# The Q, K, V projection of the next tile spread over steps 0 to 2 of an attention unit instead of 0 and 1

## The reference

```python
xn = _ln(x) * (1 + sc_msa[:, None, :]) + sh_msa[:, None, :]
qkv = xn @ w_qkv + b_qkv                      # 576 -> 3 x 16 heads x 36
q = _ln(q, g_q)                               # over the 36 entries of a head
k = _ln(k, g_k)
attn = softmax(einsum('bhqd,bhkd->bhqk', q, k) * HD ** (-0.5))
o = einsum('bhqk,bhkd->bhqd', attn, v) ... @ w_proj + b_proj
x = x + g_msa[:, None, :] * o
h = gelu((_ln(x) * (1 + sc_mlp) + sh_mlp) @ w1 + b1)
x = x + g_mlp[:, None, :] * (h @ w2 + b2)
```

## Time and profile before

| | us |
|---|---|
| median of three runs | 2977.52 (2975.45 to 2980.61) |
| the profiled execution's own time | 2975.9 |
| its span, first to last instruction | 2974.1 |
| PE busy | 2791.4 (94%) |
| DVE busy | 2008.1 (68%) |
| ACT busy | 1535.3 (52%) |
| POOL busy | 690.3 (23%) |

### The profile page before, as it was taken

One profiled execution on the slowest core, in us unless ns is written; L12 is line 12 of the kernel. 1 busy time (PEld: TensorE's weight loads), 2 busy tenths in 40 slices (PEclk: granted clock), 3 DMA queues, 4 the chain that ended last, 5 costly groups with the idle time before them and its releaser, 6 DMA issues. The chain is left out here.

```text
span 2974.1 us, 43644 instructions
## 1 busy us (share of the span) xinstructions
PE 2791.4 (94%) x14764; PEld 1441.4 (48%) x14764; DVE 2008.1 (68%) x2665; ACT 1535.3 (52%) x2211; POOL 690.3 (23%) x496
## 2 busy tenths in 40 slices
PE   4579999999999999999999999359999999999999
PEld 1334444444444444444444444126675766757666
DVE  5568888888888888888888899565344353443521
ACT  2457777778877777777777777342112111121110
POOL 0143256632233343333333310010000000000000
PEclk9789999999999999999999999669999999999999
DMA  5142223222211111111111100451202112021100
GB/s 168 64 84 52 53 65 82 72 64 50 50 37 34 31 31 33 29 34 28 34 28 33 30 13 14 146 166 34 80 7 85 54 32 85 9 78 54 33 17 17
DMA packets 201780, 157.00 MB, mean 53 GB/s; under 512 B 146982, under 2 KB 147494, under 8 KB 201522
## 3 DMA queue, kind: packets, MB, share of 16 engines
q1 hardware_dynamic: 199976, 152.17, 18.6%
q10 hardware_dynamic: 1676, 3.02, 0.3%
HBM read 87.49 MB, written 34.09 MB: 41 GB/s over the span
## 5 line engine op out<-in xcount | busy, mean ns | idle before, releaser
L705 DVE TENSOR_TENSOR at_plo<-at_p 128x1024 fp32r<-128x1024 f32 x1024 | 1266.9, 1257 | 215.8 <-ACT at_p L616 206.6
L616 ACT ACTIVATE at_p<-at_ps 128x1024 f32<-128x1024 f32 x1024 | 1048.3, 1026 | 424.9 <-PE at_ps L833 423.8
L845 PE MATMUL at_ps<-at_plo,at_vr 128*37 128x512 f32 x2048 | 1070.7, 590 | 0.0
L842 PE MATMUL at_ps<-at_p,at_v 128*73 128x512 bf16 x2048 | 796.3, 389 | 0.4 <-DVE at_plo L705 0.3
L1288 PE MATMUL ml_ps<-ml_w2s,ml_hid 128*128 128x288 f16 x3456 | 429.8, 287 | 2.0 <-issue 2.0
L1309 PE MATMUL ml_ps<-ml_xhi,ml_w 128*128 128x512 f16 x1296 | 400.9, 382 | 11.9 <-ACT ml_g L1139 9.0
L1288 PEld LDWEIGHTS ml_ps<-ml_w2s,ml_hid 128*128 128x128 f16 x3456 | 338.7, 98 | 87.9 <-issue 2.5
L842 PEld LDWEIGHTS at_ps<-at_p,at_v 128*73 128x73 f16 x2048 | 232.7, 114 | 239.8 <-DVE at_plo L705 1.7
L845 PEld LDWEIGHTS at_ps<-at_plo,at_vr 128*37 128x37 f32 x2048 | 233.6, 114 | 221.3
L525 POOL TENSOR_TENSOR at_tssq<-at_tssq,head_eps 128x8 f32<-128x8 f32 x112 | 124.1, 1108 | 925.2 <-DVE at_tssq L679 925.2
L861 PE MATMUL at_ps<-wq,at_xhi 128*128 128x432 f16 x1008 | 297.1, 350 | 19.1 <-DVE at_txc L683 18.6
(11 more groups left out here) (157 smaller groups left out, 2317.6 us busy)
## 6 DMA issues: line engine op xcount, KB each, us to landing
head_sums<-at_oT SPq DMA_DIRECT2D x256, 72.0 KB
ml_held<-head_sums SPq DMA_DIRECT2D x64, 256.0 KB
at_xy<-in_x SPq DMA_DIRECT2D x32, 288.0 KB, 2.8
ml_x<-in_x SPq DMA_DIRECT2D x8, 1152.0 KB, 5.6
out<-ml_x SPq DMA_DIRECT2D x7, 1152.0 KB, 4.5
wm<-in_L_cond_w_mod SPq DMA_DIRECT2D x6, 1152.0 KB, 14.3
ml_hid<-in_L_cond_w SPq DMA_DIRECT2D x5, 1152.0 KB, 5.6
ml_held<-head_rden SPq DMA_DIRECT2D x24, 216.0 KB
```

The source lines that it names most:

```text
L616: act.activation(p[:, s % NP, :], ps[:, 2 * (s % 2):2 * (s % 2) + 2, :].rearrange("p a n -> p (a n)"), ACT.Exp).then_inc(exp_done, 1)
L705: nc.vector.tensor_tensor(plo[:, s % NP, :], p[:, s % NP, :], high, ALU.subtract).then_inc(plo_ready, 1)
L842: nc.tensor.matmul(acc[0:VW, bass.ds((U % 2) * CH, CH)], v16[:, h % 2, 2 * s + a, 0:VW], high, start=(s == 0 and a == 0), stop=False, skip ...
L845: last = nc.tensor.matmul(acc[0:RW, bass.ds((U % 2) * CH, CH)], vr[:, h % 2, 2 * s + a, 0:RW], plo[:, s % NP, a * CH:(a + 1) * CH], start= ...
```

## The change

Three schedules written by hand are shifted. On PE the fourteen products of a tile stand in steps 0, 1 and 2 as 5, 5 and 4, where they stood in steps 0 and 1 as 7 and 7. On ACT `tile_v` moves from step 2 to 3 and `tile_square` from 3 to 4. On DVE `tile_sum` moves from step 3 to 4 and `tile_normal` from 6 to 7. POOL's `tile_power` follows by its semaphore. The number of instructions, their operands and their waits stay as they are.

```diff
 (ACT)
-                    if fresh and s == 2:
+                    if fresh and s == 3:
                         tile_v(X, row)
-                    if fresh and s == 3:
+                    if fresh and s == 4:
                         tile_square(X)
 (DVE)
-                    if fresh and s == 3:
+                    if fresh and s == 4:
                         tile_sum(X)
-                    if fresh and s == 6:
+                    if fresh and s == 7:
                         tile_normal(X)
 (PE)
-                    if fresh and s < 2:
-                        tile_products(U + 1, ..., range(7 * s, 7 * s + 7))
+                    if fresh and s < 3:
+                        tile_products(U + 1, ..., range(5 * s, min(5 * s + 5, 14)))
```

More of the change, by code:

```diff
@@ L934, in attend @@
                         sums(U - 1, (h - 1) % GH if fixed and qc == 0 else h, s - LAG + STEPS)
-                    if fresh and s < 2:
-                        tile_products(U + 1, 0 if at_end else u + 1, G + (2 if at_end else 1), range(7 * s, 7 * s + 7))
+                    if fresh and s < 3:
+                        tile_products(U + 1, 0 if at_end else u + 1, G + (2 if at_end else 1), range(5 * s, min(5 * s + 5, 14)))
                     if G == HATS_IN and s == 4:
```

## The result

The changed kernel takes 3090.11 us (median of four runs, 3088.46 to 3091.39) against 2978.39 for the kernel before, measured in alternation with it: 1.0375 times as long, 95% interval 1.0357 to 1.0393. That is 111.7 us; 108.8 were forecast. (The forecast of 3086 counted from 2977.52, the median of the first three runs before; a fourth makes it 2978.39.) The profiled execution of the changed kernel takes 3091.4 us.

The account below looks back on a forecast made before the run. PE, laid end to end, bounds the kernel. Terms of 71.8 + 17.8 + 18.2 + 1.0 = 108.8 us on the profiled 2975.9 give 3084.7, and 1.6 more for the median gives 3086 us, range 3068 to 3106.

Parts of the forecast that it names:

- What bounds the kernel; the slack: Attention: PE's work is laid end to end; a plain unit has 0.19 us to spare between normalisation and next product.
- The change on PE: Products in steps 0 to 2: step 3 keeps its distance from the first product; one more switch per unit costs 1 us.
- The later sum: DVE's sum, now behind the subtraction of step 4, starts 1.11 us later in a plain unit.
- The two paths: From sum to normalisation: through POOL it starts at 1209.19, through DVE behind step 7's subtraction at 1209.04; the later counts.
- plain (groups 1, 3 to 6): 78 plain units: PE waits 0.92 us in step 0 of each, 71.8 us.
- group 0: 16 tiles with no slack left: the whole 1.11 us of the later sum reaches PE, 17.8 us.
- group 2: 16 tiles: step 7's subtraction delays the normalisation by one pitch of 1.14 us, and PE waits already: 18.2 us.
- That POOL is not what ends last: Plain units: the power takes 1.64 us, DVE's path decides with a wait of 0.77 us; 3075 us, chance 0.15.
- That POOL shuts DVE out: Step 7's subtraction is lengthened by 0.72 us or held until the power ends: 3131 or 3173 us, chance 0.07.
- That every fourth unit collides with `head`: In 27 units `head` on POOL runs beside normalisation and gain, 19 us on top: 3106 us, chance 0.06.
- Not slower: Earlier scores 1 and 2 carry through to steps 4 and 7, so PE would not wait: 2973 us, chance 0.02.

Follow-up runs that it names:

- experiment 7: Kernel before with one more POOL addition of 128x8, result unused, in front of its own: 3054.25 us, ratio 1.0257.
- experiment 1: Kernel before with only PE's products spread as 5, 5, 4 over steps 0 to 2, ACT and DVE as before: 2976.74 us, ratio 0.9997.
- experiment 3: Changed kernel with the normalisation back behind the subtraction of step 6, sum and square still one step late: 3052.14 us, ratio 1.0249.
- experiment 5: Changed kernel with POOL's addition and power replaced by one addition of constants, normalisation behind the subtraction of step 7: 3078.13 us, ratio 1.0334.
- experiment 6: Changed kernel with POOL's addition and power replaced by one addition of constants and the normalisation behind the subtraction of step 6: 2975.85 us, ratio 0.9993.
- experiment 4: Changed kernel with the products as 7 and 7 in steps 1 and 2, so the first product is later too: 2971.00 us, ratio 0.9973.

## Why the prediction was right

**What bounds the kernel; the slack.** Right. PE back to back with 0.19 us to spare in a plain unit: experiment 7 measures it at 0.22 by lengthening one path, and the changed kernel itself gives 0.22 as well (1.11 by the later sum and 0.09 by the longer power, of which 0.98 arrive).

**The change on PE.** Costed at 1 us; experiment 1 finds 1.2 us less than before with 0 inside the interval, so no run shows this term. The step that mattered, that step 3 keeps its distance from the first product, holds.

**The later sum.** Forecast 1.11 us. From the tile's first load to the sum it is now 1268.38 - 1258.90 = 9.48; before it was 8.39 (1203.83 less the load of that tile at 1195.44): 1.09 in this unit, 1.11 in the mean of the plain ones.

**The two paths.** Right in both parts. In plain units POOL ends last; experiments 3, 5 and 6 show each path by itself. DVE's would end 0.25 earlier by experiment 5, where 0.15 were forecast (the idle 0.16 in front of the normalisation is less than that, since in these rows the normalisation starts 0.09 before the subtraction ends when nothing holds it). The term that was a little too small lies here: the power takes 2.59 instead of 2.50, and sum to normalisation 4.34 instead of 4.25. The prediction had what it takes to see it. It found that the power would start 0.13 into subtraction 6, as it starts inside subtraction 5 today, and took the same 2.50. Today it starts 0.22 into it, and what is left of the subtraction counts (see the hardware section).

**The terms.** They can be read off as distances between first product loads, from that of tile 1 to that of tile 111. Before:

```profile
184.75 0.13 PEld L861 LDWEIGHTS at_ps<-wq,at_xhi 128*128 128x128 f16 x2 [16.42 <-DVE at_txc L683]
...
1679.83 0.11 PEld L861 LDWEIGHTS at_ps<-wq,at_xhi 128*128 x2 [0.34 <-issue]
```

After:

```profile
187.25 0.13 PEld L861 LDWEIGHTS at_ps<-wq,at_xhi 128*128 128x128 f16 x2 [16.42 <-DVE at_txc L683]
...
260.88 0.11 PEld L861 LDWEIGHTS at_ps<-wq,at_xhi 128*128 x2 [1.54 <-issue]
275.52 0.11 PEld L861 LDWEIGHTS at_ps<-wq,at_xhi 128*128 x2 [1.54 <-issue]
...
698.55 0.11 PEld L861 LDWEIGHTS at_ps<-wq,at_xhi 128*128 x2 [1.71 <-issue]
713.79 0.11 PEld L861 LDWEIGHTS at_ps<-wq,at_xhi 128*128 128x128 f16 x2 [1.61 <-DVE at_txc L683]
...
1792.25 0.11 PEld L861 LDWEIGHTS at_ps<-wq,at_xhi 128*128 x2 [1.32 <-issue]
```

1605.00 against 1495.08: 109.9 us in 110 units. By the same distances at the ends of the groups:

| | units | forecast | measured |
|---|---|---|---|
| plain (groups 1, 3 to 6) | 78 | 71.8 | 76.3 |
| group 0 | 16 | 17.8 | 17.5 |
| group 2 | 16 | 18.2 | 16.1 |
| products cut in three | | 1.0 | in the above |

The plain term was 6% too small, 0.98 us a unit against 0.92: 0.09 by the longer power, less what every fourth unit saves (its load follows the normalisation by 0.05 and not by 0.15, as at 713.79 above, behind a normalisation that ends at 713.74). In group 3 the load follows by 0.24 or more in most units (941.10 behind a normalisation that ends at 940.85), some 1 us in all; the first product waits for one more semaphore there (`n_lo`), and whether that is why was not tried. The term of group 2 was 2 us too large, because it took an ordinary unit for all sixteen. Before the change every fourth one was already some 0.5 us longer; after it all take 15.2 to 15.3 us. The subtraction in front of the normalisation shows where the 0.5 came from. Beside two casts of `head` it takes 1.76 us in such a unit, 1.23 otherwise:

```profile
657.63 1.76 DVE L705 TENSOR_TENSOR at_plo<-at_p 128x1024 fp32r<-128x1024 f32 x1 [1.06 <-ACT at_p L616]
...
657.64 0.67 POOL L518 CAST at_v<-at_v 128x576 f16<-128x576 f32 x1
```

The plain term was thus 4.5 us too small and the other three together 3.4 too large. That the sum comes within 1.1 us of the 109.9 is in part luck. Of the 115.5 us between the two spans, 2.5 lie ahead of the first of these loads and 3.1 behind the last; what they are was not tried. The medians are 111.7 apart: the profiled execution before lies 2.5 us under its median and the one after 1.3 above, so some of it is the scatter between runs.

**The rivals.** That POOL is not what ends last: no, the power was 2.59 and not 1.64. Without the power the loss would be 12 us smaller, close to the 11 at which this rival was priced, but only because `head` then collides (experiment 5). That POOL shuts DVE out: no; the three subtractions up to the normalisation take 3.81 us, of which 0.14 are the wait for exponential 7. That every fourth unit collides with `head`: no, in the plain groups of the changed kernel those are not longer than the others. Before the change in group 2, and in experiment 5, some are, by 0.5 and 0.4 us. Not slower: no; exponential 7 starts 11.37 behind the tile's first load (1270.27 and 1258.90), where it started 11.39 behind it before (1206.83 and 1195.44), and experiment 4 shows what it takes, a later first product.

## What to carry to other kernels

A schedule that shifts a chain of hand-overs by a step has to shift its first consumer as well: here the reader of a single PSUM bank went one step later, and the next writer of the bank did not, so some 0.2 us of slack in 78 units, and none in 32, met 1.1 us of delay. Before moving a step for balance, look for the resource that closes the loop and subtract the end of its last reader from the start of its next writer: that difference, taken from one unit's timeline, predicted the loss within 3%, with some luck in how the errors of the terms fell. And where two paths of nearly the same length lead to a wait, shortening one gives back only the difference between them (12 of 112 us here), so both have to be costed before either is blamed.

## What the runs showed of the hardware

A POOL operation that starts within a DVE subtraction takes longer, by about what is left of the subtraction. In group 2 after the change the addition of 128x8 found DVE between subtractions and took 0.20 us; in plain units, beside one, it takes 1.11:

```profile
708.07 0.45 DVE L679 TENSOR_REDUCE at_tssq<-at_txc 128x8 f32<-128x288 f32 x1
708.70 1.23 DVE L705 TENSOR_TENSOR at_plo<-at_p 128x1024 fp32r<-128x1024 f32 x1 [0.19 <-ACT at_p L616]
...
708.59 0.20 POOL L525 TENSOR_TENSOR at_tssq<-at_tssq,head_eps 128x8 f32<-128x8 f32 x1 [6.33 <-DVE at_tssq L679]
708.87 2.55 POOL L527 TENSOR_TENSOR at_tssq<-at_tssq,power 128x8 f32<-128x8 f32 x1
```

The power then starts at 708.87, within the subtraction at 708.70, and takes 2.55 where it took 1.64 before the change in this group. The subtractions in which the power starts in a plain unit, before and after the change:

```profile
1205.32 1.22 DVE L705 TENSOR_TENSOR at_plo<-at_p 128x1024 fp32r<-128x1024 f32 x1
...
1269.97 1.23 DVE L705 TENSOR_TENSOR at_plo<-at_p 128x1024 fp32r<-128x1024 f32 x1
```

Three rows, one relation: with 1.00 us of the subtraction left (1205.54 to 1206.54) the power takes 0.86 more than 1.64, with 1.06 left (708.87 to 709.93) 0.91 more, with 1.10 left (1270.10 to 1271.20) 0.95 more. It is what is left less some 0.15.

When the power comes first, nothing of the sort is seen. In group 2 before the change a subtraction starts 0.03 behind it, and neither is drawn out:

```profile
655.29 1.64 POOL L527 TENSOR_TENSOR at_tssq<-at_tssq,power 128x8 f32<-128x8 f32 x1
...
655.32 1.25 DVE L705 TENSOR_TENSOR at_plo<-at_p 128x1024 fp32r<-128x1024 f32 x1 [0.16 <-ACT at_p L616]
```

Beside POOL's casts of 128x576 a subtraction does get longer (1.76 at 657.63 above).

The Trainium skill (SBUF — State Buffer, Who interferes with whom) says that a DVE instruction with two SBUF inputs contends with a GpSimd instruction that reads SBUF, that the ports they share are an exclusive lock, and that the order of issue, not the shape of the operation, decides who blocks. The trace agrees where DVE came first (1.11 against 0.20, 2.55 against 1.64) and beside the casts, and not where a running power would have to hold DVE back (1.25 at 655.32).
